# Cross-attention layer on one core: order of the last projections, of the last reciprocal and transpose, and the banks of the last output tiles

## What is computed

```python
qh = _split_heads(q @ Wq.T + bq)          # q: (4, 2048, 512), 16 heads of 32
kh = _split_heads(k @ Wk.T + bk)          # k = v = context: (4, 77, 512)
vh = _split_heads(v @ Wv.T + bv)
scores = jnp.einsum('bhqd,bhkd->bhqk', qh, kh) / scale
scores = jnp.where(mask == 0, -1e9, scores)
m = jnp.max(scores, axis=-1, keepdims=True)
e = jnp.exp(scores - m) * mask
probs = e / (jnp.sum(e, axis=-1, keepdims=True) + 1e-09)
attn = jnp.einsum('bhqk,bhkd->bhqd', probs, vh)
out = attn.transpose(0, 2, 1, 3).reshape(4, 2048, 512) @ Wo.T + bo
x = out + q
mu = x.mean(-1); var = ((x - mu) ** 2).mean(-1)
return (x - mu) / sqrt(var + 1e-05) * ln_g + ln_b
```

## Time and profile before

| | us |
|---|---|
| median of 3 runs (lowest, highest) | 602.46 (601.54, 602.71) |
| the profiled execution, its own time | 604.55 |
| its span, first to last instruction | 602.8 |
| TensorE busy in the span | 568.3 (94%) |
| VectorE busy | 528.6 (88%) |
| ScalarE busy | 501.3 (83%) |
| GpSimd busy | 436.9 (72%) |
| mean granted TensorE clock | 0.979 of full speed |

### The profile page before, as it was taken

One profiled execution on the slowest core, in us unless ns is written; L12 is line 12 of the kernel. 1 busy time (PEld: TensorE's weight loads), 2 busy tenths in 40 slices (PEclk: granted clock), 3 DMA queues, 4 the chain that ended last, 5 costly groups with the idle time before them and its releaser, 6 DMA issues.

```text
span 602.8 us, 15264 instructions
## 1 busy us (share of the span) xinstructions
PE 568.3 (94%) x5460; PEld 461.3 (77%) x5460; DVE 528.6 (88%) x803; ACT 501.3 (83%) x2284; POOL 436.9 (72%) x401
## 2 busy tenths in 40 slices
PE   3978888999999999999999999999999999998894
PEld 3866666787878788787878788887878788786673
DVE  4586998899999989898999989898999989899776
ACT  4339979889989999899979998899979997899421
POOL 3223677368695886799777985799777986797797
PEclk9989888999999999999999999999999999999798
DMA  8558220220325201730145212520425212302142
GB/s 306 157 181 252 108 81 11 72 82 3 128 71 216 72 18 58 250 124 21 47 149 196 90 54 75 200 87 3 151 76 197 82 53 102 110 19 88 73 140 104
DMA packets 36198, 64.91 MB, mean 108 GB/s; under 512 B 12443, under 2 KB 14491, under 8 KB 34075
## 3 DMA queue, kind: packets, MB, share of 16 engines
q1 hardware_dynamic: 35979, 63.94, 31.2%
q10 hardware_dynamic: 144, 0.00, 0.0%
HBM read 44.15 MB, written 19.46 MB: 106 GB/s over the span
## 4 chain that ended last, share of the span: by engine, by line
PE 84%; DVE 8%; DMA 3%; SPq 2%; issue 2%; ACT 0%; DVEq 0%; POOL 0%
PE qo_bank L534 28%; PE qo_bank L430 26%; PE s_bank L430 17%; PE av_bank L520 10%; DVE E L854 1%; DVE WoT_lo L811 1%; PE av_bank L445 1%; PE s_bank L534 1%; DMA TP<-in_WvT 1%; DMA K_scratch<-TP 1%; DVE TP L883 1%; SPq L318 1%; DVE bn L906 1%; PE av_bank L430 1%; DMA E<-in_ctxT 1%
## 5 line engine op out<-in xcount | busy, mean ns | idle before, releaser
L678 ACT ACTIVATE E<-E,neg_max 128x77 f32<-128x77 f32 x1024 | 352.4, 354 | 30.2 <-DVE neg_max L862 30.2
L678 ACT ACTIVATION_READ_ACCUMULATOR E<-E,neg_max 128x1 f32 x1024 | 198.6, 194 | 0.0
L1165 POOL TENSOR_TENSOR E<-E,inv_sum 128x1232 f32<-128x1232 f32 x64 | 145.3, 2278 | 40.7 <-DVE inv_sum L869 40.7
L854 DVE TENSOR_TENSOR E<-s_bank,mask_bias 128x616 f32<-128x616 f32 x128 | 101.2, 791 | 23.2 <-PE s_bank L430 21.6
L430 PE MATMUL s_bank<-Kd,QT_hi 128*128 128x308 f32 x512 | 112.8, 307 | 0.0
L862 DVE TENSOR_REDUCE neg_max<-E 128x8 f32<-128x624 f32 x128 | 99.4, 783 | 0.4
L883 DVE STREAM_TRANSPOSE TP<-E 128x1280 f32<-128x1280 f32 x64 | 95.0, 1494 | 1.0 <-issue 0.6
L430 PE MATMUL s_bank<-Kd,QT_lo 128*128 128x308 f32 x256 | 81.9, 320 | 12.7 <-DVE E L854 12.7
L430 PEld LDWEIGHTS s_bank<-Kd,QT_hi 128*128 128x128 f32 x512 | 85.5, 191 | 4.4
L1183 POOL TENSOR_TENSOR Y<-Y,b_row 128x512 f32<-128x512 f32 x62 | 79.5, 1304 | 3.6 <-ACT Y L695 3.5
L1156 POOL TENSOR_TENSOR Y<-Y,bo_row 128x1024 f32<-128x1024 f32 x32 | 77.2, 2428 | 0.0
(11 more groups left out here) (71 smaller groups left out, 831.7 us busy)
## 6 DMA issues: line engine op xcount, KB each, us to landing
Y<-in_x SPq DMA_DIRECT2D x16, 1024.0 KB, 5.4
out_y<-Y SPq DMA_DIRECT2D x64, 256.0 KB, 2.0
xT_raw<-in_xT SPq DMA_DIRECT2D x15, 1024.0 KB, 6.3
Vp<-V_scratch SPq DMA_DIRECT2D x32, 96.0 KB, 2.3
K_scratch<-TP SPq DMA_DIRECT2D x1, 1232.0 KB, 5.6
xT_raw<-in_xT SPq DMA_DIRECT2D x2, 512.0 KB, 7.1
Y<-in_WqT SPq DMA_DIRECT2D x4, 256.0 KB, 9.3
TP<-in_WvT SPq DMA_DIRECT2D x4, 256.0 KB, 5.3
```

The lines of the kernel that those rows point to most:

```text
L678: last = cp(e, e, ACT.Exp, bias=neg_max[:, t, h:h + 1], accum_out=rowsum[:, t, h:h + 1])
L854: tt(E[:, t, :, 0:SK].rearrange("p (g j) k -> p g j k", g=2), s_bank[:, :, 0:GK].rearrange("p g (j k) -> p g j k", j=HG), mask_bias[:, row ...
L1165: nc.gpsimd.tensor_tensor(out=e, in0=e, in1=inv.unsqueeze(2).broadcast_to((P, 2 * HH, SK)), op=ALU.mult).then_inc(probs_ready, 1)
```

## The change

1. **Half projections.** `OUT_first(14, 2)` and `OUT_first(14, 3)`, into the score banks, go directly behind the last scores `S(15, 7)`, ahead of `OUT(13, 2)`. `OUT_first(14, 0)` goes from ahead of `AV(15, 0)` to behind `AV(15, 1)`.
2. **VectorE's turn 17.** The last reciprocal `inverse(15, 3)` and `turn(15, 2)` go ahead of `residual(13, 2)`, and `turn(15, 3)` directly behind that residual, ahead of its `stats`.
3. **Banks of block 15.** The four `OUT(15, k)` write into the four attention banks; they no longer wait for `centered` of an earlier projection.

```diff
-                    20: (("OUT", 14, 1),),
-                    21: (("OUT", 15, 0), ("OUT", 15, 1), ("OUT", 15, 2), ("OUT", 15, 3))}
+                    20: (("OUT", 14, 1),)}
...
+        def last_out(o):
+            return o == NB - 1
+
         def out_bank(o, k):
+            if last_out(o):
+                return av_bank[:, k, :]
             return s_bank[:, k - 2, :] if split_out(o) and k >= 2 else qo("OUT", o, k)[:, :]
...
-                qo_free("OUT", o, k)
+                if not last_out(o):
+                    qo_free("OUT", o, k)
...
                 elif s == 19:
-                    S(15, 7), OUT(13, 2), OUT(13, 3), OUT_first(14, 0), AV(15, 0), AV(15, 1)
+                    S(15, 7), OUT_first(14, 2), OUT_first(14, 3), OUT(13, 2), OUT(13, 3), AV(15, 0), AV(15, 1)
                 elif s == 20:
-                    OUT_first(14, 1), OUT(14, 0), OUT(14, 1)
+                    OUT_first(14, 0), OUT_first(14, 1), OUT(14, 0), OUT(14, 1)
                 elif s == 21:
-                    OUT_first(14, 2), OUT_first(14, 3), OUT(14, 2), OUT(14, 3), OUT(15, 0), OUT(15, 1)
+                    OUT(14, 2), OUT(14, 3), OUT(15, 0), OUT(15, 1)
                     OUT(15, 2), OUT(15, 3)
...
                 elif s == 17:
-                    inverse(15, 2), turn(15, 0), turn(15, 1), residual(13, 2), inverse(15, 3), stats(13, 2)
-                    aggregate(13, 2), turn(15, 2), center(13, 2), turn(15, 3), residual(13, 3), stats(13, 3)
+                    inverse(15, 2), turn(15, 0), turn(15, 1), inverse(15, 3), turn(15, 2), residual(13, 2)
+                    turn(15, 3), stats(13, 2), aggregate(13, 2), center(13, 2), residual(13, 3), stats(13, 3)
```

More of the change, by code:

```diff
@@ L243, in xattn_program @@
         QO_PLACE = {unit: n for n, unit in enumerate(QO_ORDER)}
-        assert len(QO_ORDER) == len(QO_PLACE) == 8 * NB - 2
+        assert len(QO_ORDER) == len(QO_PLACE) == 8 * NB - 6
         def qo(kind, b, i):
```

## The result

| | before | changed |
|---|---|---|
| median (lowest, highest), 18 runs each | 602.43 (601.36, 604.97) | 600.83 (599.26, 603.83) |
| ratio to before, 95% interval | | 0.9973 (0.996 to 0.9986) |
| span of the profiled execution | 602.8 | 600.2 |

The change saves 1.6 us (0.8 to 2.4 by the interval). The predicted time was 601.5 with a range of 600.1 to 602.9, so the measured one lies in the range, nearer to its lower end.

The account below looks back on a forecast made before the run. It took a TensorE-VectorE relay with slowed clock to bound the head, GpSimd's run the changed tail. 571.3 + 30.1 = 601.4 against 602.8 gains 1.4, or 0.4 against short-fall runs; 602.46 - 0.9 gives 601.5 us, range 600.1 to 602.9.

Parts of the forecast that it names:

- Head: From the last scores to the end of AV(15): shorter pause, one 3.4 us low-clock stretch, T at 571.3, gain 2.3 us.
- That the parts only work together: Half projections ahead of OUT(13, 2) delay the residual and turn(15,3) behind it; TensorE's work covers this by 0.5 us.
- Tail: After AV(15): GpSimd's 17.09 us run sets the end at T + 30.1 against T + 29.2, a loss of 0.9 us.
- a gain of 1.4 us: Whole span against the profiled execution: 601.4 against 602.8.
- The middle is 0.9: At OUT(13, 2): gain 1.4 us against the profile, 0.4 against runs with a short clock fall; middle 0.9.
- The forecast's own path: Last 48 us: one short clock fall and GpSimd setting the end, 601.1 to 602.1, chance 0.55.
- the rival that the clock stays up: Behind the last scores: no clock fall after the 1.82 us pause, T = 570.4, time 600.2 to 601.2, chance 0.25.
- an outcome (faster): Measured time of the whole kernel: more than 1.2 us (0.2%) below 602.46, chance 0.39.
- A wrong reading without effect: In the tail: OUT(15, 0) starts 11 us after AV(15) has ended, so using other banks costs nothing.
- The new banks: In TensorE's tail: the wait of 0.26 us for a bank of block 15 goes.

Follow-up runs that it names:

- e4: Only VectorE's new order, TensorE's order and banks as in the kernel before; ratio to before 1.0028 (1.0013 to 1.0043).
- e3: TensorE's new order and the new banks, VectorE's order as in the kernel before; ratio to before 1.0034 (1.0021 to 1.0047).
- e5: The whole change, with tile (15,1) finished on VectorE too; ratio to the kernel before 0.9932 (0.9911 to 0.9953).
- e2: Only block 15's tiles moved to the attention banks, all orders as in the kernel before; ratio to before 0.9989 (0.9968 to 1.001).
- e12: VectorE's new order alone against the kernel before, timed a second time; ratio to before 1.0019 (0.9995 to 1.0042).
- e1: Both new orders, TensorE's and VectorE's, but block 15 keeps the shared banks; ratio to the kernel before 1.0001 (0.9982 to 1.0019).
- e9: The whole change with tile (15,1) finished on VectorE too, run again; ratio to the kernel before 0.997 (0.9953 to 0.9986).
- e11: The whole change with bias(15,7) ahead of block 13's two stats, profiled again; 46.6 us from last scores to span end, no timing of its own.
- e7: The whole change plus tile (15,1) finished on VectorE and bias(15,7) moved early; ratio to the kernel before 0.9964 (0.994 to 0.9988).
- e6: The whole change, with bias(15,7) ahead of the two stats of block 13 on VectorE; ratio to the kernel before 0.9954 (0.993 to 0.9979).

## Why the prediction was right

- **Head.** Predicted: pause 1.82 us, low clock for 3.4 us, normalise done 9.3 us after the last scores, T 15.8 us after them (571.3 - 555.46). Measured: 1.83, 3.4, 9.3 and 15.91. TensorE itself, not the turn, releases AV(15), by 0.6 us (0.5 predicted). That the pause had to be filled for this is not shown, as said behind e4.
- **That the parts only work together.** The prediction said that the half projections are not free, as the residual stands between the turns. e3 shows the price: without VectorE's order they make the kernel slower than before. e4 shows the other side: VectorE's order alone gains nothing, as OUT_first(14, 0) and its wait stand ahead of AV(15).
- **Tail.** Predicted: inv_std of (15, 2) at T + 25.1, over 2 us of waiting ahead of finish_row, the end at T + 30.1. Measured: T + 24.9 (595.24 - 570.32), 2.44 us, T + 29.9. e5 shows the bound by moving it. GpSimd's run took 16.96 us from first to last inv_std; from before, the spacing of starts had said 17.09 and the added durations 16.8. Within the changed run the durations add up to 16.7, again 0.3 less than the spacing, so the 0.3 is time that does pass; the spacing came out a little shorter than before, mostly since the four add_beta took 4.92 us and not 5.00. TensorE ends at T + 19.9 where the prediction had T + 20.2: the wait for a bank was worth more than its 0.26.
- **Against its own execution** the forecast was a gain of 1.4 us. D fell by 1.5 (47.3 to 45.8; 45.9 by the prediction's numbers).
- **The term that was mis-sized** is the last one: "The middle is 0.9". I took off half a microsecond because the runs of before might mostly have a low stretch of 3.4 us at OUT(13, 2), as at 83 us, where the profile had 6.8. The pause of 3.33 us has been profiled four times (before, e2, e4, e12): AV(15) started 14.2 us after the last scores each time, and the low stretch behind it lasted 6.8 us in all four, so the discount had nothing behind it. Without it the forecast would have been 602.46 - 1.4 = 601.1 against 600.83 measured.
- **What the number owes to luck.** The forecast's own path was given 601.1 to 602.1, mostly less than 1.2 us of gain, and 0.52 went to a gain too small to tell from none. The measured 600.83 lies outside that span. It falls into the 600.2 to 601.2 of the rival that the clock stays up, though the clock fell. The two timings (1.6 and 1.3 us) are both clear of no change and over that 1.2, an outcome (faster) that had 0.39. The mechanism was right; the middle was half a microsecond off by the discount, and the wide range took that in.
- **A wrong reading without effect.** OUT(15, 0) does not start 11 us after AV(15) has ended but 8.5 (578.83 - 570.32; 10.0 in before). It still starts without a wait.
- **The new banks** I had costed by a wait of 0.26 us. By themselves they are worth 0.5 (e2), and within the change they are worth all of it (1.6 us by the timings, 2.0 by D, e1), since without them the wait grows to 2.6 us and pulls the clock down. The total was right, as the banks were in the change, but my account of what they do was not. That is the other term that was mis-sized.
- **The rival that the clock stays up** had 0.25. The pause of 1.83 us has been profiled six times (the change twice, e1, e3, e5, e9), and in all six the clock fell once behind it, for 3.4 us.

## What to carry to other kernels

At the end of a kernel, where engines hand over to each other, add up each engine's own remaining run from its first possible start: here an engine with 0% of the chain had half a microsecond of room, and as soon as the busiest one was relieved it took 0.7 of the 2.2 us back. Moves that free different engines are worth trying together, since leaving one out took the gain away (e1, e3) and one alone brought 0.5 us or nothing (e2, e4). A change of several moves should also be tried without each of them: the half projections were not, and by the rows they may bring nothing. And a wait on TensorE is to be costed with the clock behind it: at the end of this kernel the pauses of 1.7 to 3.3 us that a fall of the clock followed cost another 1.4 to 2.7 us of half speed (5.41 against 4.02 us, 5.50 against 2.79), and moving a pause to another place moved this cost too.

## What the runs showed of the hardware

- A pause of the same length can be followed by a fall of the clock or not: 1.72 us ahead of AV(15), with 0.9 us some 10 us earlier, left AV(15) at 4.02 us in two profiles and made it about 5.4 in two others. Behind the last scores, pauses of 0.9 us were followed by no fall before that one, in four profiles; pauses of 1.83 us (six), 2.41, 2.60 and 3.33 us (four) in the last 50 us were followed by one each time.
- Earlier in the same kernels this is no rule. Ahead of scores between 80 and 83 us, pauses of 1.93 to 1.98 us were followed by a fall in four profiles (before, e4, e9, e11), pauses of 1.84 and 2.03 us by none in two (e7, e6). TensorE and the clock in e6:

```profile
80.47 0.41 PE L434 MATMUL s_bank<-Kd,QT_lo 128*128 128x308 f32 x1 [2.03 <-DVE E L859]
```
```profile
83.00:84.00 1.00, 1.00 (x6) 0.77 (x6) 0.54 (x2) 1.00 (x7) 0.00 (x0) 1.00 1.00 375
```

- Behind the pause of 3.33 us the low stretch lasted 6.8 us, four times of four; behind the shorter ones of the last 50 us it lasted 3.4 us. The length of the pause alone doesn't set it: near 34 us a pause of 3.44 us in before was followed by 3.4 us, and near 67 us one of 1.75 us in the changed kernel (with one of 0.89 some 2 us behind it) by 6.8.
- The last scores end between 552.0 and 556.3 us in profiles of kernels that are the same up to there. Of this spread I can only say that the low stretches of the first 110 us differ too (6.8 us in sum in e6, 13.7 in before); its cause stays open. It is wider than any effect looked for here, so D and T inside one execution told more than medians did.
